# A graph layer with layer norm on one core: GpSimd's gathers held to TensorE's progress, pairwise statistics, fewer register loads, biases ahead of scales

## What is computed

```python
src, tgt = x[row], x[col]
h = relu(concat([src, tgt, edge_attr]) @ W1 + b1)
msg = h @ W2 + b2
attn_weight = sigmoid(concat([msg, conf]) @ Wa + ba)
out = segment_sum(msg * attn_weight, col, num_segments=x.shape[0])
x = layernorm(x + out)        # (x - mean) / sqrt(var + 1e-5), over 128 values
```

## Time and profile before

| | us |
|---|---|
| median of 3 runs | 693.69 (690.98 to 698.72) |
| span of the profiled execution | 792.5 |

### The profile page before, as it was taken

The page is one execution under the profiler, slowest core; times in us unless marked ns, Lnnn a source line. Parts: engine busy times, 40 slices in busy tenths (PEclk is TensorE's granted clock), DMA queues, the critical chain, the costliest instruction groups (busy, mean ns, idle before and its releaser), DMA issues. The chain is left out here.

```text
span 792.5 us, 8991 instructions
## 1 busy us (share of the span) xinstructions
PE 425.7 (54%) x1902; PEld 299.8 (38%) x1902; DVE 502.9 (63%) x2146; ACT 427.9 (54%) x1089; POOL 457.6 (58%) x473
## 2 busy tenths in 40 slices
PE   1842778463764136763646566656463475543560
PEld 0531545332543123643435254444251254322250
DVE  5944988878793228883667579888461995330542
ACT  0433686678963047691546567757641698520360
POOL 7676572665666756464755735575746366467330
PEclk9985988777786558985887767977866889776785
DMA  7946678888886226685576568886754657431120
GB/s 190 357 133 208 224 273 299 279 293 254 268 305 207 84 82 219 241 297 171 173 241 199 184 221 264 291 281 232 253 160 133 234 159 233 117 116 59 35 59 14
DMA packets 79882, 159.37 MB, mean 201 GB/s; under 512 B 13970, under 2 KB 48086, under 8 KB 79826
## 3 DMA queue, kind: packets, MB, share of 16 engines
q1 hardware_dynamic: 65106, 129.47, 48.8%
q0 software_dynamic: 14720, 29.32, 13.1%
HBM read 99.75 MB, written 59.95 MB: 202 GB/s over the span
## 5 line engine op out<-in xcount | busy, mean ns | idle before, releaser
L887 PE MATMUL hid_ps<-turned,w 128*128 128x512 f32 x294 | 184.1, 776 | 102.4 <-issue 52.8
L741 ACT ACTIVATE turned<-turn_ps 128x512 f32<-128x512 f32 x147 | 80.3, 590 | 193.5 <-remote 130.0
L760 ACT ACTIVATE nodes<-nodes,sc 128x128 f32<-128x128 f32 (+1 forms) x462 | 184.0, 485 | 0.0
L641 POOL DMA_INDIRECT rows_src<-x,src_list x132 | 131.8, 998 | 85.4 <-issue 36.9
L662 POOL DMA_INDIRECT out<-stash,row_idx x132 | 131.3, 994 | 75.8 <-issue 40.2
L652 POOL DMA_INDIRECT rows_dst<-x,dst_list x132 | 125.8, 953 | 82.8 <-issue 36.2
L1186 DVE BATCH_NORM_STATS2 stats<-nodes 128x6 f32<-128x128 f32 (+1 forms) x693 | 152.8, 278 | 7.7 <-DMA nodes<-x 5.7
L887 PEld LDWEIGHTS hid_ps<-turned,w 128*128 128x128 f32 x294 | 69.6, 253 | 179.7 <-issue 126.5
L921 PE MATMUL sum_ps<-gated,place 128*128 128x128 f32 x384 | 69.1, 342 | 113.6 <-DVE near L1313 62.2
L897 PE MATMUL msg_ps<-w2x,hid 128*128 128x129 f32 x392 | 69.1, 331 | 108.0 <-ACT hid L746 71.4
L921 PEld LDWEIGHTS sum_ps<-gated,place 128*128 128x128 f32 x384 | 60.7, 241 | 131.5 <-DVE near L1313 65.8
(11 more groups left out here) (146 smaller groups left out, 510.1 us busy)
## 6 DMA issues: line engine op xcount, KB each, us to landing
nodes<-x SPq DMA_DIRECT2D x62, 704.0 KB
out<-nodes SPq DMA_DIRECT2D x62, 704.0 KB
attr_in<-edge_attr SPq DMA_DIRECT2D x49, 256.0 KB
near_dst<-line SPq DMA_DIRECT2D x16, 256.0 KB
near_x<-x SPq DMA_DIRECT2D x20, 192.0 KB
near_x<-x SPq DMA_DIRECT2D x24, 128.0 KB
out<-near SPq DMA_DIRECT2D x4, 704.0 KB
rows_src<-x,src_list POOLq DMA_INDIRECT x132
```

Of the source, the lines that this page charges most:

```text
L641: pool.indirect_dma_start(out=rows_src[:, k % RING, j, :], out_offset=None, in_=x[:, :], in_offset=bass.IndirectOffsetOnAxis(ap=idx[:, j:j ...
L741: act.activation(turned[:, k % 2, c], turn_ps[:, c], ACT.Copy).then_inc(turned_ready, 1)
L760: return act.activation(row, row, ACT.Identity, scale=sc[0:parts, b % 2, 0, col:col + 1], bias=sc[0:parts, b % 2, 1, col:col + 1])
L887: last = pe.matmul(hid_ps[:], w1[:, c, :], turned[:, k % 2, c, :], start=(c == 0), stop=(c == 2))
```

## The change

- GpSimd: the pause goes. `gather_src(k)` now waits until the whole of `turn(k-2)` is done (AHEAD = 2) in place of the source part of `turn(k-4)`. The ring of four buffers stays.
- VectorE's statistics: one `bn_stats` reads two rows interleaved (`p w f -> p f w`), so that its even and odd halves are the statistics of one row each. A lone last row is read twice by a broadcast. Of a batch's 33 rows in three chunks, the last row of the second chunk is paired with the first row of the third. `scales` no longer joins the two halves: nine chained operations in place of thirteen.
- The four registers of a near step (VectorE's and SyncE's) come with one load of several registers and no bounds assert.
- In VectorE's loop `add_bias(k)` stands ahead of the near statistics and `scales`.
- ScalarE's and VectorE's counts of normalised rows share a semaphore, and the start sets its limits with fewer `memset`s.

```diff
-PAUSE = 2
+AHEAD = 2
-SSTEPS = 13
+SSTEPS = 9
@@ gpsimd
             def gather_src(k):
-                if k >= RING:
-                    pool.wait_ge(turned_ps_ready, 3 * (k - RING) + 1)
+                if k >= AHEAD:
+                    pool.wait_ge(turned_ps_ready, 3 * (k - AHEAD) + 3)
                 for j in range(G):
-                    pause(j)
                     pool.indirect_dma_start(
...
-                group_begun(src_got[k % RING], 16 * G * (k // RING + 1), 2)
@@ sync
-                for j in range(G):
-                    base = sp.value_load(base_row[0:1, g * G + j:g * G + j + 1], min_val=0, max_val=N - 4 * P)
+                bases = loaded(sp.engine, base_row[0:1, g * G:(g + 1) * G], N - 4 * P)
+                for j, base in enumerate(bases):
@@ vector
+        def loaded(engine, row, most):
+            _, values = nc.values_load_multi_w_load_instructions(
+                row, engines=(engine,), min_val=0, max_val=most,
+                skip_runtime_bounds_check_because="VectorE holds the row between its bounds when it makes it")
+            return values
...
-                then(dve.tensor_tensor(mean2, mean_e, mean_o, ALU.add), False)
-                then(dve.tensor_tensor(apart, mean_e, mean_o, ALU.subtract), False)
-                then(dve.tensor_tensor(v, m2_e, m2_o, ALU.add))
-                then(dve.scalar_tensor_tensor(a, apart, F / 4.0, apart, ALU.mult, ALU.mult))
-                then(dve.scalar_tensor_tensor(v, v, F * EPS, a, ALU.add, ALU.add))
+                then(dve.tensor_scalar(v, m2, F * EPS, None, ALU.add))
...
+            def pair_stats(st, rows):
+                pair = rows.rearrange("p w f -> p f w")
+                if rows.shape[1] == 1:
+                    pair = pair.to_broadcast([rows.shape[0], F, 2])
+                return dve.bn_stats(st.rearrange("p w k -> p (w k)"), pair)
+
+            def pair_rows(b, i):
+                if i == 1 and crosses(b):
+                    return (0, 2, 4, 6, 8, 10)
+                if i == 2 and crosses(b):
+                    return (1, 3, 5, 7, 9)
+                return (0, 2, 4, 6, 8, 10)
...
+                if k < K:
+                    add_bias(k)
                 if (k % 2 == 0 or k == K) and b < BATCHES and k <= K:
...
-                if k < K:
-                    add_bias(k)
```

More of the change, by code:

```diff
@@ L132, in list_groups_of, with even, crosses, node_column @@
     return [STEPS[k - 1][1] for k in (2 * b - 1, 2 * b) if is_list(k - 1)]
+def even(n):
+    return n + n % 2
+def crosses(b):
+    return 3 * b + 2 < 62
+def node_column(b, i, r):
+    before = 0 if i == 0 else even(ROWS) + (i - 1) * (ROWS if crosses(b) else even(ROWS))
+    return COLS[b]["nodes"] + before + r
 def columns(b):
@@ L139, in columns @@
         at["nodes"] = n
-        n += TRIO * ROWS
+        n += even(ROWS) + (2 * ROWS if crosses(b) else 2 * even(ROWS))
     for i in list_groups_of(b):
@@ L145, in columns @@
         at["near"] = n
-        n += NEAR_OUT[b][1] - NEAR_OUT[b][0]
+        n += even(NEAR_OUT[b][1] - NEAR_OUT[b][0])
     return at, n
@@ L769, in norm_chunk @@
                 for r in range(ACT_ROWS[i]):
[L770 to L771 removed]
+                    last = norm(nodes[0:n, c % SLOTS, r, :], b, node_column(b, i, r), n)
+                last.then_inc(normed[c % SLOTS], 1)
             def norm_list(b, i):
@@ L784, in norm_near @@
                     last = norm(near[:, low + r, :], b, COLS[b]["near"] + r)
-                last.then_inc(near_act_normed, 1)
+                last.then_inc(near_normed, 1)
             act.wait_ge(consts_in, 16 * 8)
@@ L1003, in _ @@
             step(dve.memset(b2_all[:, F:F + 1], 0.0))
[L1005 to L1010, removed]
+            for row, of in enumerate((lambda g: FINAL[g] - KA[g], lambda g: LOW if g >= 14 else 0,
+                                      lambda g: P * KG[g], lambda g: P * KA[g])):
+                first = 0
+                for g in range(1, DG + 1):
+                    if g == DG or of(g) != of(first):
+                        step(dve.memset(limit[0:1, row, first * G:g * G], float(of(first))))
+                        first = g
             step(dve.memset(limit[0:1, 0, DT:DT + 1], float(NB - 1)))
@@ L1185, in stat_row @@
                     dve.wait_ge(x_landed[u], 16 * (c // SLOTS + 1))
-                ins = dve.bn_stats(stats[0:n, b % 2, COLS[b]["nodes"] + i * ROWS + r, :], nodes[0:n, u, r, :])
-                if r == ROWS - 1:
+                crossing = r == ROWS - 1 and i == 1 and crosses(b)
+                if crossing:
+                    dve.wait_ge(x_landed[(c + 1) % SLOTS], 16 * ((c + 1) // SLOTS + 1))
+                w, row = node_column(b, i, r), u * ROWS + r
+                wide = 1 if r == ROWS - 1 and not crossing else 2
+                ins = pair_stats(stats[0:n, b % 2, w:w + 2, :], every_row[0:n, row:row + wide, :])
+                if r >= ROWS - 2:
                     ins.then_inc(stat_ready, 1)
@@ L1198, in norm_row @@
                 if r == ROWS - 1:
-                    ins.then_inc(dve_normed[u], 1)
+                    ins.then_inc(normed[u], 1)
             def list_stats(i, b):
                 dve.wait_ge(stashed, i + 1)
-                for j in range(G):
-                    last = dve.bn_stats(stats[:, b % 2, COLS[b][i] + j, :], stash[:, list_slot(i) + j, :])
+                for j in range(0, G, 2):
+                    w, row = COLS[b][i] + j, list_slot(i) + j
+                    last = pair_stats(stats[:, b % 2, w:w + 2, :], stash[:, row:row + 2, :])
                 last.then_inc(stat_ready, 1)
@@ L1210, in near_stats @@
                 dve.wait_ge(v_added, 1)
-                for r in range(high_ - low_):
-                    last = dve.bn_stats(stats[:, b % 2, COLS[b]["near"] + r, :], near[:, low_ + r, :])
+                for r in range(0, high_ - low_, 2):
+                    w = COLS[b]["near"] + r
+                    last = pair_stats(stats[:, b % 2, w:w + 2, :], near[:, low_ + r:min(low_ + r + 2, high_), :])
                 last.then_inc(stat_ready, 1)
@@ L1301, in sum_near @@
                 n, width = near_number(g), KA[g]
-                blocks = [dve.value_load(block_row[0:1, g * G + j:g * G + j + 1], min_val=0, max_val=NB - width)
-                          for j in range(G)]
+                blocks = loaded(dve.engine, block_row[0:1, g * G:(g + 1) * G], NB - width)
                 if n == 0:
```

59 lines of the change are left out of this document (21 added, 38 removed).

## The result

The changed kernel takes 635.84 us (median of 4 runs, 632.47 to 637.77) and the kernel before, timed beside it, 695.53 us: a ratio of 0.913, with a 95% interval of 0.908 to 0.918. Forecast were 668 us, 3.7% less than before; it became 8.7% less. The profiled run took 637.77 us, with a span of 636.0 us.

A forecast was written before the change was run, and what follows sets the result against it. It took VectorE's work, 25.0 us for two steps, and TensorE stalls under GpSimd's unbroken issuing as bounds, GpSimd as the new one. 693.7 - 32 (pace) - 13 (stalls) + 19 (end) = 668 us; range 650 to 686, 8 in 10 634 to 706.

The forecast's parts named there:

- VectorE's statistics and scales, 24 + 16 us: VectorE: paired statistics at 0.325 us a pair save 24 us, one operation in the scales' chain saves 16 us.
- the rival with a dear read: VectorE's interleaved read is slow, or gathers come too late: +35 in place of -24 us, some 705 us; chance 6%.
- The register loads, 14 us: Near steps: one load of four registers saves 1.65 us each, 26 us, about half hidden in the sequencer: 14 us.
- Pace, -32 us: Step loop: VectorE's savings shorten two steps, held by GpSimd's floor of 23.7 us from step 15 on: 21 + 11 us.
- Biases ahead of scales: VectorE's loop: gates go first, against ScalarE's 5.77 us wait for the logit in even steps; no extra sum counted.
- Gathers held to two steps back: GpSimd's gathers: rows still in time by 2 to 12 us, no cost; 13 of 26 us of stalls gone.
- The end, +19 us: Last steps: 44 scatters behind `gather_src(48)` make 72 us from the end of `turn(46)` against 53.4; costs 18.6, bounds 10 to 35.
- Stalls are most of it: Rival: the 26 us are all stalls, the pair reaches GpSimd's floor, the end costs 10: 638 us; chance 22%.
- GpSimd streams and nothing is gained: Rival: pace stays at 12.5 us as breaks in GpSimd's stream let TensorE through: 695 us; chance 15%.
- The end grows: Rival: the last 44 unbroken scatters hold TensorE in steps 47 and 48, +48 us: 722 us; chance 17%.
- The sign of no run of over some 20 DMAs: Sign of being right: GpSimd issues no run of over some 20 DMAs without a break before the last scatters.
- the sign of being wrong: TensorE waiting at L861 or L866 for rows; also listed: `bn_stats` over 0.4 us, or two steps above 25 us with GpSimd idle.

The follow-up runs named there:

- before_again: The kernel before, unaltered, profiled once more: 696.32 us, span 694.6 us.
- before_gpsimd: The kernel before without the pause and with gathers waiting for the whole of step k-2, VectorE as before: 639.01 us, ratio 0.925.
- after_old_gpsimd_2: The changed kernel with GpSimd's old program (pause, wait for step k-4), run again at the usual level: 703.75 us, ratio 1.013 to the kernel before.
- before_no_pause: The kernel before with only the pause taken away, the wait for step k-4 kept: 627.81 us, ratio 0.908.
- after_ring_single_loads: The changed kernel with the wait for step k-4 and one register a load: 630.71 us, ratio 0.908 to the kernel before.
- before_no_pause_2: The kernel before with only the pause taken away, repeated on another chip: 630.12 us, ratio 0.909.
- before_ahead_2: The kernel before with its pause, the wait for step k-2 in place of k-4 as only edit, run again: 698.91 us, ratio 1.008.
- after_old_gpsimd: The changed kernel with GpSimd's old program (pause, wait for step k-4), in the slow session: 769.68 us, ratio 0.985 to the kernel before.

## Why the prediction was wrong

**The failed step** is the sentence "Taking the pause away gains nothing by itself: GpSimd sat 68.7 us waiting for TensorE anyway." Taken away alone, it gave 66 us. The step rests on three readings of the first profile. The pause "held it for 0.24 us only": that is one pause of some 57. The landing rows of the same view came to 48.8 us there and 96.9 in before_again, and were never added up. And the 68.7 us of slack were that profile's own, taken where TensorE was late; in before_again they are 0.6 us. The prediction did see that the profile ran 98.8 us over the timed runs, and then priced stalls by it (13 of 26 us) and put the pause's worth in the same trace at nothing. That profile could carry neither.

**VectorE's statistics and scales, 24 + 16 us.** The durations were about right and worth nothing. A pair was forecast at 0.325 us a start (and the 442 starts taken away are 444 by the pages):

```profile
188.09 1.08 DVE L1169 BATCH_NORM_STATS2 stats<-nodes 128x6 f32<-128x256 f32 x3
```

That is (1.08 - 0.42) / 2 = 0.33 us, so the interleaved read costs nothing of its own, and the rival with a dear read is out. VectorE's busy time fell by 37.7 us (499.1 to 461.4). At most 3 us of it reached the end (before_gpsimd against the changed kernel). With the pause it turned into VectorE's wait for messages (76.1 us in before_again, 141.6 in after_old_gpsimd_2); without it, VectorE's wait is 15.0 us in before_no_pause and 65.6 in the changed kernel, and TensorE's for rows 11.5 and 69.5.

**The register loads, 14 us.** The row of the load of four, in the queue of VectorE:

```profile
L433 DVEq TENSOR_LOAD <-block_row x16: 340/348/1470, 58.1 to 586.2; - x16
```

It takes 0.348 us against 0.304 for one, and less than the 0.3 + 0.55 us that I took. On SyncE the same load is dearer:

```profile
L433 SPq TENSOR_LOAD <-base_row x16: 299/872/1137, 17.3 to 560.6; - x16
```

That is 0.872 us, where a load of one took 0.270 in before_again, so three more registers cost 0.60 us there and 0.04 on VectorE. The Trainium skill ("Runtime: NRT & Kernel Launch", Instruction fetch mechanics) has some 200 ns a register in bulk, for registers loaded from HBM: SyncE's row agrees, though this row of numbers lies in SBUF; VectorE's, from SBUF as well, doesn't. Neither is seen in the time: after_ring_single_loads, with a load for each register, is no slower.

**Pace, -32 us.** The floor was rightly placed at GpSimd's 28 DMAs for three steps, but the kernel before was thought to stand above it for VectorE's sake. It stood above it for the pause's waits, 96.6 us in 40 recorded waits of about 2.4 us each. The right sum starts from GpSimd's account of a profile at the timed level: 695 less 97 of landings, plus gaps uncovered, plus new waits.

**Biases ahead of scales.** The even steps' wait for the logit, 5.77 us in the earlier trace rows, is gone where I looked (no wait ahead of the weights at 177.24 us), and over all 49 steps ScalarE waits 30.0 us for it, where before_no_pause_2 has 55.9. The time had no gain of it, rather the unsettled 3 us of loss.

**Gathers held to two steps back.** Forecast at nothing for late rows; it costs 11 us in the old kernel and 3 or less in the changed one. It is the wait of GpSimd, not that of TensorE, that is paid. The 13 us of stalls that the nearer wait was to cure weren't there: with the pause kept it lost 4 us (before_ahead_2), and no "remote" wait stands in before_again.

**The end, +19 us.** The 72 us from the end of `turn(46)` came out about right by luck: it ends at 561.0 and the span 75.0 us later, but GpSimd didn't wait for it. `gather_src(48)` starts at 562.9, 0.31 us after the DMA before it, when its turn in the stream comes. As a loss against before it was wrong: at the usual level the kernel before ends with the same scatters, not with ScalarE as in the earlier trace rows, so nothing hidden was uncovered.

**The rivals.** "Stalls are most of it" gave 638 us, the nearest number, for a reason that the runs don't bear out: the stalls weren't in the timed runs. "GpSimd streams and nothing is gained" had the mechanism half: GpSimd does stream, its last 352 DMAs with one gap of 0.37 us among those of 0.30, and that is the gain. "The end grows" fell: 44 scatters without a break, and steps 47 and 48 went on beside the first of them, TensorE's last sums by 589.7. That GpSimd, with 58% of the span (74% with its issue gaps), was the bound already, by its pauses, stood among no rivals.

**The signs.** The span fell by 156.5 us and the time by 60, as foretold, but because the first profile was slow. The scatters are the last work and the "remote" waits are gone, in before_again as well. The sign of no run of over some 20 DMAs failed (180 in a row from 163 us on), and the sign of being wrong, TensorE waiting for rows at L860 and L865, came: 67.4 us, though before_again has 151.9 at the same places.

**The best version** of these is the changed kernel with the wait for step k-4 and the biases behind the scales (626.21 and 630.38 us, 0.902 and 0.907), with the kernel before without its pause next to it (0.908 and 0.909), within what the runs can tell.

## What to carry to other kernels

Before any sum, compare the profile's span with the timed runs; where they are 14% apart, get the waits from a profile at the timed level, or give every term that rests on a wait both signs. For each engine that issues in order add busy time, issue gaps and each class of wait up to the span: an engine at 58% can be the one whose every wait is paid. And work saved on an engine that then waits longer is no term of the sum, however well its duration is known.

## What the runs showed of the hardware

- An indirect DMA of 128 rows occupies GpSimd some 0.97 to 1.01 us with 0.30 us to the next, over 352 of them in a row in before_no_pause. The loads of nodes landed after 6.3 us there and after 6.6 us in before_again with its pauses, the stores after 4.9 and 4.4.
- A wait for the landing of the latest indirect DMAs, put into that stream some 57 times, cost 96.6 us of waiting; without it the kernel went from 694 to 628 us.
- One kernel, the one before, took 694 us in most sessions and 792 us in one, on a chip that gave 694 us later, with DMA queues as busy in microseconds as ever (SyncE's queue: 50.4% of 764.8 us is 385 us in after_old_gpsimd, 60.1% of 636.0 is 382 in the changed kernel). In the slow session ScalarE and VectorE waited for results with no recorded cause.
- A load of four registers took 0.87 us on SyncE against 0.27 for one, and 0.35 us on VectorE against 0.30.
- A `bn_stats` over two interleaved rows of 128 starts every 0.33 us, against 0.193 for one row.
